# Four-part transformer stack on one core: the products of constants in TensorE's stream are taken out ahead of the last unit

## The chip, the cores and the metric

The kernel runs on one core of one Trainium2 chip. The core has a matrix engine (TensorE, PE in the rows, its weight loads PEld), VectorE (DVE), ScalarE (ACT), GpSimd (POOL) and SyncE (SP), which issues most transfers. Each engine works through its own list of instructions in order and waits on semaphores for the others. The metric is the device time of one execution in microseconds (us), lower is better; the median of several executions is what is compared.

## The reference

Four blocks follow each other on x of shape (4, 1024, 256), all in float32, each as x = x + layernorm(block(layernorm(x))):

```python
def _encoder_layer(x, Wq, ..., ln2_b):                 # block 1: four of these, linear attention, 16 heads
    h = _layernorm(x, ln1_s, ln1_b)
    q, k, v = [(h @ W + b).reshape(b, t, H, DK) ...]
    qp, kp = jax.nn.elu(q) + 1.0, jax.nn.elu(k) + 1.0
    kv = jnp.einsum('bshd,bshm->bhmd', kp, v); ksum = jnp.sum(kp, axis=1)
    z = 1.0 / (jnp.einsum('blhd,bhd->blh', qp, ksum) + EPS_ATTN)
    attn = jnp.einsum('blhd,bhmd,blh->blhm', qp, kv, z).reshape(b, t, d)
    x = x + (attn @ Wo + bo)
    h = _layernorm(x, ln2_s, ln2_b)
    return x + jax.nn.relu(h @ W1 + b1) @ W2 + b2
# block 2: gate = softmax(x @ gate_w.T); out = x @ weight.T + (1/16) * sum over 8 adapters of gate * (x U^T) V^T
# block 3: Mamba: x @ W_in, causal conv of 4, silu, a recurrence over time with 16 states for each of 512 channels
def step(h, inp):
    u, d, b, c = inp
    h = h * jnp.exp(d[..., None] * A) + (d * u)[..., None] * b[:, None, :]
    return (h, jnp.einsum('bds,bs->bd', h, c))
# block 4: top-1 mixture of 8 experts (256 -> 1024 -> 256), up to 320 tokens in each, weighted by the gate
```

## The kernel before

**Tiling.** The 4096 tokens are four batches `b` of 1024, each in four groups `g` of 256 rows. Batch by batch the four encoder layers `l` run on the groups (64 groups of work in all), then block 2 (`mix`), and the result goes to DRAM. Block 3 works in eight units `u` of 512 tokens, two for each batch: its input products (`unit_input`), 64 steps (16 states times 4 channel tiles: ACT makes the decay at L1736, DVE scans at L1233 and multiplies at L1245, POOL makes products at L1991 and adds at L2004), then its output, its gate and the sorting of tokens to experts (`unit_output`). The units of batch b run beside the encoder of batch b+1. Units 6 and 7 have no encoder beside them; there TensorE adds the step's products itself (L825). When the last unit is done, the eight experts run (`expert_up`, `expert_down`).

**Order.** Each engine's list is fixed when the program is built. The work is written as generators that yield due times out of tables of numbers (`ENC`, `BASE_A`, `UNIT`, `OUT_PE` and so on), and `weave` always lets the generator with the earliest due time write its next piece. Nothing is decided on the chip: an engine that meets an unmet semaphore stands, and all behind it stands too.

**The products of constants.** Some pieces of TensorE's stream start with `n` products of the identity with itself, written into the PSUM bank that the piece has just been given and overwritten by it. Nothing reads them. They come after the wait for the bank and ahead of the wait for the data:

```python
def transposes(bank, src, order, freed, ready, spare=0):
    if freed:
        pe.wait_ge(*freed)
    idle(spare, bank)
    for semaphore, value in ready:
        pe.wait_ge(S(semaphore), value)
    for m, (t, k) in enumerate(order):
        ins = pe.transpose(bank[:, m * 128:(m + 1) * 128], src[:, t, k * 128:(k + 1) * 128], C["ident"][:])

def idle(n, bank):
    for _ in range(n):
        pe.matmul(bank[:, 0:128], C["ident"][:], C["ident"][:], start=True, stop=True, skip_group_check=True)
```

The identity is a slice of `pack0`, so the rows call them L461, `ps<-sb_pack`, and each float32 product is two records there (a transpose, L455, is one). Their numbers stand in tables, one entry for a batch and group or for a unit. `WARM_AT` stands ahead of the first product of queries with `kvm` (L602) of a group, in each of the four layers; `WARM_TR2` ahead of the transposes of the attention's result (`attended`, L455); `WARM_TR3` ahead of the transposes for the feed-forward part; `WARM_MIX` and `WARM_MIX3` (group 3) in `mix`, at its first transposes, ahead of L706 and ahead of the transposes at L718; `WARM_IN` ahead of the transposes of a unit's input (L455 on `sb_px`); `WARM_OUT` and `WARM_TR1` are all zero; `WARM_END` stands behind the last unit.

What the neighbours in the rows are: L583 sums keys times values into the bank from which DVE masks `kvm` (L1090, L1094); L1112 on DVE is the attention's result `sb_xh`, normed; L1488 on ACT is the last step of a layernorm, on which the transposes wait; L1867 on POOL is the same for a unit's input `sb_px`; L680 is the feed-forward's second product; L468 is the three-part product of split float32 operands (`mm3`).

Of the kernel before, what the change touches and what calls it, by code (L numbers as in the profile page):

```python
# [125 lines left out]
LATE = NU - 2  # L126

WARM_TR1 = ((0, 0, 0, 0), (0, 0, 0, 0), (0, 0, 0, 0), (0, 0, 0, 0))
WARM_AT = ((4, 3, 0, 0), (8, 1, 0, 0), (4, 0, 0, 0), (4, 0, 0, 0))
WARM_TR2 = ((0, 0, 1, 0), (0, 0, 1, 2), (0, 0, 1, 0), (8, 0, 1, 0))  # L130
WARM_TR3 = ((0, 0, 0, 0), (0, 0, 0, 0), (0, 0, 0, 0), (2, 0, 0, 0))
WARM_MIX = ((6, 0, 2, 0), (7, 0, 2, 0), (7, 0, 2, 0), (11, 0, 2, 0))
WARM_MIX3 = ((6, 4, 0, 0), (6, 0, 0, 0), (6, 0, 0, 0), (8, 0, 0, 0))
WARM_IN = ((6, 0, 0), (6, 0, 0), (6, 0, 0), (4, 0, 0), (6, 0, 0), (6, 0, 0), (6, 0, 0), (7, 0, 0))
WARM_OUT = ((0, 0, 0, 0), (0, 0, 0, 0), (0, 0, 0, 0), (0, 0, 0, 0), (0, 0, 0, 0), (0, 0, 0, 0), (0, 0, 0, 0), (0, 0, 0, 0))
WARM_END = (18, 22, 20, 6, 20, 22)

# [37 lines left out]
def build(nc, a, out):  # L175
    outer = ExitStack()
    with outer:
        sems = {}

        def S(name):  # L180
            if name not in sems:
                sems[name] = outer.enter_context(nc.semaphore("s_" + name))
            return sems[name]
# [182 lines left out]
        def tail(b, g, off):  # L366
            return ENC[b] + (L * LAYER + TAIL[b][g] + TAILS * off) * SLOW[b]
# [28 lines left out]
        def loads(b, n):  # L396
            return 48 * b + 16 * n - (16 if b or n > 1 else 0)
# [48 lines left out]
        def pe_program(pe):  # L446
# [9 lines that stand above are left out]
                return ins  # L456
# [5 lines that stand above are left out]
# [56 lines left out]
            def features(which, pos, when):  # L518
                for b, l, g in groups:
# [6 lines left out]
                                     ((f"d_x{g}", loads(b, 2)) if loaded else (f"lna_g{g}", j + 1),),  # L526
                                     spare=(WARM_TR1 if which == "tr1" else WARM_TR3)[b][g])
                    ins.then_inc(S(which), 1)
# [59 lines left out]
            def attend():  # L588
                for b, l, g in groups:
                    k = place(b, l, g)  # L590
                    for t in range(2):
# [5 lines left out]
                        if t == 0:  # L597
                            idle(WARM_AT[b][g], bank)
                        pe.wait_ge(S("qe"), k + 1)
# [7 lines left out]
            def attended():  # L607
                for b, l, g in groups:
# [3 lines left out]
                    where["tr2", k] = bank  # L612
                    ins = transposes(bank, xh[at(b, g)], by_t, freed, (("an", 2 * k + 2),), spare=WARM_TR2[b][g])
                    ins.then_inc(S("tr2"), 1)
# [70 lines left out]
            def mix(g):  # L685
                for b in range(NB):
                    r, j = 4 * b + g, norm(b, MIX)
                    spare = (WARM_MIX3 if g == 3 else WARM_MIX)[b]
                    yield tail(b, g, 0.0) + MIXED[b][0]
# [47 lines left out]
            def unit_input():  # L737
                for u in range(NU):
                    for k in range(2):
# [3 lines left out]
                        ins = transposes(bank, pxs[u], [(t, k) for t in range(4)], freed,  # L743
                                         (("lnp_p", 3 * u + 3), ("lna_p", 2 * u + 2)), spare=WARM_IN[u][0] if k == 0 else 0)
                        ins.then_inc(S("win"), 1)
                        ring.give(bank, S("pt"), 2 * u + k + 1)
                    for c in range(4):
# [5 lines left out]
                        if c == 0:  # L753
                            idle(WARM_IN[u][1], bank)
                        pe.wait_ge(S("pt"), 2 * u + 2)
# [21 lines left out]
                    if freed:  # L777
                        pe.wait_ge(*freed)
                    idle(WARM_IN[u][2], bank)
                    pe.wait_ge(S("xi"), 8 * u + 8)  # L780
# [1679 lines left out]
```

## Time and profile before

| | |
|---|---|
| median of 3 runs | 2798.64 us |
| lowest, highest | 2791.62, 2802.93 us |
| profiled execution, first to last instruction (span) | 2801.1 us |
| TensorE / weight loads busy | 85% / 70% of the span |
| DVE / POOL / ACT busy | 65% / 62% / 58% |
| granted TensorE clock, mean | 0.921 |
| products of constants, all | 924 records, 462 instructions |
| of these behind 2616 us | 216 records, 108 instructions |

The profiled execution is one execution, and its span lies 2.5 us above the median of the runs. Busy shares are of the whole span; TensorE's count a product from its start to its modelled end, so neighbouring products overlap in them, and the distance from one start to the next is what a product takes from the engine's time. PEclk is the clock that TensorE was granted, 1.00 being 2.4 GHz and 0.50 being 1.2 GHz.

### The profile page before, as it was taken

The numbers are of one execution on the slowest core, as the hardware profiler recorded it, in microseconds if no ns is written. First come the engines' busy times: TensorE is split into PE (matmuls) and PEld (weight loads), VectorE is DVE, ScalarE is ACT, GpSimd is POOL, SyncE is SP. The second block draws the span as 40 slices with busy tenths as digits, with TensorE's granted clock in tenths as the row PEclk, the third lists the DMA queues.
The fourth block names the chain that finished last, engine by engine and source line by source line (L and its number), as shares of the span: only waits on it lengthen the run. The fifth ranks groups of instructions, "written<-read, shape, count | busy, mean of one in ns | idle before, by whom it ended". The sixth has DMA issues, their size and how long they took to land. (4 is left out here: it accounts for less than half of the span.)

```text
span 2801.1 us, 40293 instructions
## 1 busy us (share of the span) xinstructions
PE 2391.1 (85%) x13172; PEld 1965.7 (70%) x13172; DVE 1810.1 (65%) x3883; ACT 1618.4 (58%) x3649; POOL 1723.6 (62%) x1988
## 2 busy tenths in 40 slices
PE   6999998899989858798989887989898766666898
PEld 5889987687869755686878756877788532122698
DVE  4232334678677774887378667784777766879566
ACT  4555666677656654666476655766666556523153
POOL 1111214298659873898369847985598755778356
PEclk8999999999979988899999998999999878778899
DMA  4435233223413232232223133232221232323142
GB/s 159 170 139 192 95 116 135 92 63 104 120 63 95 69 120 88 72 112 66 100 65 113 50 132 100 77 114 74 78 91 46 72 119 73 81 81 88 47 146 93
DMA packets 123899, 273.85 MB, mean 98 GB/s; under 512 B 9213, under 2 KB 64125, under 8 KB 114092
## 3 DMA queue, kind: packets, MB, share of 16 engines
q1 hardware_dynamic: 120108, 263.37, 29.4%
q0 software_dynamic: 3584, 7.92, 0.8%
q8 instruction: 107, 1.75, 0.3%
q14 instruction: 100, 0.82, 0.1%
HBM read 215.93 MB, written 58.48 MB: 98 GB/s over the span
## 5 line engine op out<-in xcount | busy, mean ns | idle before, releaser
L1991 POOL TENSOR_TENSOR sb_sc<-sb_bc,sb_du 128x512 f32<-128x512 f32 x512 | 660.8, 1296 | 107.6 <-issue 38.3
L2004 POOL TENSOR_TENSOR sb_ya<-sb_ya,sb_sc 128x512 f32<-128x512 f32 x384 | 494.8, 1289 | 27.3 <-DVE sb_sc L1245 27.1
L680 PE MATMUL ps<-sb_w,sb_fa 128*128 128x256 f32 x2048 | 494.2, 385 | 5.2 <-ACT sb_fa L1601 5.2
L468 PE MATMUL ps<-sb_hT,sb_w 128*128 128x256 f32 x2048 | 405.2, 297 | 15.7 <-issue 5.9
L680 PEld LDWEIGHTS ps<-sb_w,sb_fa 128*128 128x128 f32 x2048 | 376.6, 193 | 49.8 <-ACT sb_fa L1601 3.9
L1736 ACT ACTIVATE ps<-sb_dl,sb_aneg 128x512 f32<-128x512 f32 x512 | 349.9, 687 | 99.3 <-DVE sb_sc L1245 91.0
L1233 DVE TENSOR_TENSOR_SCAN ps<-ps,sb_sc 128x512 f32<-128x512 f32 x240 | 292.9, 1224 | 101.5 <-ACT ps L1736 94.1
L468 PEld LDWEIGHTS ps<-sb_hT,sb_w 128*128 128x128 f32 x2048 | 329.2, 193 | 34.5 <-issue 23.2
L1233 DVE TENSOR_TENSOR_SCAN ps<-ps,sb_hl,sb_sc 128x512 f32<-128x512 f32 x240 | 306.8, 1283 | 67.2 <-ACT ps L1736 63.2
L1245 DVE TENSOR_TENSOR sb_sc<-ps,sb_bc 128x512 f32<-128x512 f32 x480 | 321.8, 671 | 0.0
L1601 ACT ACTIVATE sb_fa<-ps,sb_b1n 128x256 f32<-128x256 f32 x512 | 209.8, 464 | 147.3 <-PE ps L468 146.9
L468 PE MATMUL ps<-sb_hL,sb_w 128*128 128x256 f32 x1024 | 292.4, 286 | 0.0
L1876 POOL TENSOR_SCALAR sb_g_rs<-sb_g_ss 128x2 f32<-128x2 f32 x148 | 30.1, 204 | 323.0 <-ACT sb_xh L1480 316.8
L825 PE MATMUL ps<-sb_sc,sb_pack 128*128 128x512 f32 x256 | 160.8, 745 | 76.5 <-DVE sb_sc L1245 61.6
L455 PE MATMUL ps<-sb_pack,sb_xh 128*128 128x128 f32 x832 | 134.9, 289 | 101.6 <-ACT sb_xh L1488 86.5
L468 PE MATMUL ps<-sb_wq,sb_hT 128*128 128x512 f32 x512 | 198.9, 430 | 19.7 <-DVE sb_b1n L1026 7.6
L1488 ACT ACTIVATE sb_xh<-sb_xb,sb_g_nm,sb_g_rs 128x256 f32<-128x256 f32 x304 | 164.9, 591 | 75.4 <-POOL sb_g_nm L1883 74.7
L468 PEld LDWEIGHTS ps<-sb_hL,sb_w 128*128 128x128 f32 x1024 | 196.3, 192 | 0.0
L455 PEld LDWEIGHTS ps<-sb_pack,sb_xh 128*128 128x128 f32 x832 | 105.0, 149 | 125.8 <-ACT sb_xh L1488 64.9
L1060 DVE TENSOR_TENSOR sb_hL<-ps,sb_hT 128x512 fp32r<-128x512 f32 x128 | 87.9, 687 | 141.5 <-ACT sb_hT L1436 140.7
L825 PEld LDWEIGHTS ps<-sb_sc,sb_pack 128*128 128x128 f32 x256 | 49.6, 224 | 182.9 <-DVE sb_sc L1245 131.0
L1878 POOL TENSOR_TENSOR sb_g_rs<-sb_g_rs,sb_mhalf 128x2 f32<-128x2 f32 x184 | 130.7, 710 | 57.1 <-DVE sb_g_nm L981 44.7
(262 smaller groups left out, 5055.1 us busy)
## 6 DMA issues: line engine op xcount, KB each, us to landing
sb_bc<-b_and_c SPq DMA_DIRECT2D x128, 512.0 KB, 5.0
sb_w<-w_parts SPq DMA_DIRECT2D x15, 2048.0 KB, 7.7
sb_wq<-w_qkv_parts SPq DMA_DIRECT2D x15, 1536.0 KB
sb_w<-in_w SPq DMA_DIRECT2D x16, 1024.0 KB
sb_raw<-in_mw SPq DMA_DIRECT2D x16, 1024.0 KB, 9.7
gate_z<-sb_xin SPq DMA_DIRECT2D x30, 256.0 KB, 2.2
sb_zt<-gate_z SPq DMA_DIRECT2D x30, 256.0 KB, 3.8
expert_in<-sb_bb SPq DMA_DIRECT2D x5, 1032.0 KB, 12.9
```

What stands on the lines that cost most here:

```text
L455: ins = pe.transpose(bank[:, m * 128:(m + 1) * 128], src[:, t, k * 128:(k + 1) * 128], C["ident"][:])
L468: ins = pe.matmul(bank, lhs[x], rhs[y], start=(first and m == 0), stop=(last and m == 2), skip_group_check=True)
L680: ins = pe.matmul(acc[:, v * D:(v + 1) * D], fa[i % 3][:, h * 256 + v * 128:h * 256 + (v + 1) * 128], w2[:, 2 * f + h, :], start=(f == 0 a ...
L825: pe.matmul(held[c][:], C["ident"], db[m % RING], start=False, stop=(s == NS - 1), skip_group_check=True).then_inc(S("adp"), 1)
L1233: v.tensor_tensor_scan(db[m % RING] if on_pool(m) else da[m % 3][:], da[m % 3][:], db[m % RING], start, ALU.mult, ALU.add).then_inc(S("sc" ...
L1245: v.tensor_tensor(db[m % RING], da[m % 3][:], bc[:, i % 3, 1, :], ALU.mult).then_inc(S("cm"), 1)
L1488: ins = e.activation(xh[at(b, g)][:, t, :], x[:, t, :], ACT.Identity, bias=nm[:, t:t + 1], scale=rs[:, t:t + 1])
L1601: ins = e.activation(fa[i % 3][:, cols], where["w1", i][:, cols], ACT.Relu, bias=b1n[:, l, 2 * f + h2:2 * f + h2 + 1])
L1736: e.activation(da[m % 3][:], dls[u][:, c, :], ACT.Exp, scale=aneg[:, c, s:s + 1]).then_inc(S("ex"), 1)
L1878: i = own.tick(p.tensor_tensor(rs[:, 0:2], rs[:, 0:2], mhalf[:, 0:2], ALU.pow))
L1991: p.tensor_tensor(db[m % RING], bc[:, i % 3, 0, :], dus[u][:, c, :], ALU.mult).then_inc(S("bm"), 1)
L2004: p.tensor_tensor(yas[u][:, c, :], yas[u][:, c, :], db[m % RING], ALU.add).then_inc(S("ad"), 1)
```

## The change

Six of the nine tables are set to zero: `WARM_AT`, `WARM_TR2`, `WARM_TR3`, `WARM_MIX`, `WARM_MIX3` and `WARM_IN`. `WARM_END` is kept. No due time and no other instruction is touched; where a block of L461 carried the wait for its bank, the first instruction behind it now carries that wait.

```diff
-WARM_AT = ((4, 3, 0, 0), (8, 1, 0, 0), (4, 0, 0, 0), (4, 0, 0, 0))
-WARM_TR2 = ((0, 0, 1, 0), (0, 0, 1, 2), (0, 0, 1, 0), (8, 0, 1, 0))
-WARM_TR3 = ((0, 0, 0, 0), (0, 0, 0, 0), (0, 0, 0, 0), (2, 0, 0, 0))
-WARM_MIX = ((6, 0, 2, 0), (7, 0, 2, 0), (7, 0, 2, 0), (11, 0, 2, 0))
-WARM_MIX3 = ((6, 4, 0, 0), (6, 0, 0, 0), (6, 0, 0, 0), (8, 0, 0, 0))
-WARM_IN = ((6, 0, 0), (6, 0, 0), (6, 0, 0), (4, 0, 0), (6, 0, 0), (6, 0, 0), (6, 0, 0), (7, 0, 0))
+WARM_AT = ((0, 0, 0, 0), (0, 0, 0, 0), (0, 0, 0, 0), (0, 0, 0, 0))
+WARM_TR2 = ((0, 0, 0, 0), (0, 0, 0, 0), (0, 0, 0, 0), (0, 0, 0, 0))
+WARM_TR3 = ((0, 0, 0, 0), (0, 0, 0, 0), (0, 0, 0, 0), (0, 0, 0, 0))
+WARM_MIX = ((0, 0, 0, 0), (0, 0, 0, 0), (0, 0, 0, 0), (0, 0, 0, 0))
+WARM_MIX3 = ((0, 0, 0, 0), (0, 0, 0, 0), (0, 0, 0, 0), (0, 0, 0, 0))
+WARM_IN = ((0, 0, 0), (0, 0, 0), (0, 0, 0), (0, 0, 0), (0, 0, 0), (0, 0, 0), (0, 0, 0), (0, 0, 0))
 WARM_END = (18, 22, 20, 6, 20, 22)
```

TensorE's stream in the first layer of batch 0, where the queries of groups 0 and 1 meet `kvm` (`s_qe` and `s_ke` are the waits for a bank, `s_kvm` the one for the masked sums):

```order
-L461 MATMUL ps<-sb_pack 128x128 [waits s_qe]
-L461 MATMUL ps<-sb_pack 128x128 x3
 L602 MATMUL ps<-sb_kvm,sb_xh 128x136 [waits s_kvm,s_qe]
 L602 MATMUL ps<-sb_kvm,sb_xh 128x136
 L602 MATMUL ps<-sb_kvm,sb_xh 128x136 [waits s_kvm,s_qe,s_ke]
 L602 MATMUL ps<-sb_kvm,sb_xh 128x136
-L461 MATMUL ps<-sb_pack 128x128 [waits s_ke]
-L461 MATMUL ps<-sb_pack 128x128 x2
-L602 MATMUL ps<-sb_kvm,sb_xh 128x136 [waits s_kvm,s_qe]
+L602 MATMUL ps<-sb_kvm,sb_xh 128x136 [waits s_kvm,s_qe,s_ke]
```

The seven products are gone, and the wait for the bank `s_ke` moved onto the L602 behind them; the L602 products follow each other in the same order.

TensorE's stream in a layer of batch 3, where the attention's result of group 0 is transposed (`s_an` counts DVE's L1112):

```order
 L602 MATMUL ps<-sb_kvm,sb_xh 128x136 [waits s_kvm,s_qe,s_an]
 L602 MATMUL ps<-sb_kvm,sb_xh 128x136
-L461 MATMUL ps<-sb_pack 128x128 [waits s_an]
-L461 MATMUL ps<-sb_pack 128x128 x7
 L455 MATMUL ps<-sb_pack,sb_xh 128x128 [waits s_an]
 L455 MATMUL ps<-sb_pack,sb_xh 128x128 x3
```

Eight products are gone between the last L602 and the transposes, and the wait stays the same one.

## Rows read from the trace of the kernel before

**Rows 1.** The cores' clock; the page's busy time and clock in 40 slices
```profile
core 0: 2801.1 us, clock 0.921
...
PE 2391.1 (85%) x13172; PEld 1965.7 (70%) x13172; DVE 1810.1 (65%) x3883; ACT 1618.4 (58%) x3649; POOL 1723.6 (62%) x1988
...
PEclk8999999999979988899999998999999878778899
```

**Rows 2.** Busy time by stretch, all engines; the column after POOL is PEclk
```profile
0.00:434.00 434.00, 403.62 (x2488) 358.92 (x2489) 145.43 (x496) 240.02 (x613) 77.00 (x201) 0.96 0.40 144
550.00:960.00 410.00, 376.18 (x2229) 330.15 (x2229) 307.07 (x603) 267.68 (x641) 323.29 (x339) 0.95 0.28 86
2330.00:2616.00 286.00, 197.61 (x380) 71.27 (x379) 235.08 (x300) 130.34 (x218) 213.26 (x196) 0.84 0.29 80
```

**Rows 3.** Line L461 alone: the whole line, and the last stretch (PE, PEld, PEclk)
```profile
L461 PE MATMUL ps<-sb_pack x924: 270/275/584, 60.7 to 2657.8; 128*128 128x128 f32 x185
...
2616.00:2801.00 185.00, 29.02 (x216) 28.21 (x216) 0.95 0.30 106
```

**Rows 4.** Order of time, layer 0 of batch 0: start, us, what, [idle before]
```profile
60.75 1.06 PE L461 MATMUL ps<-sb_pack 128*128 128x128 f32 x8
...
61.35 0.17 DVE L1094 TENSOR_TENSOR sb_kvm<-ps,sb_pack 128x16 f32<-128x16 f32 x1
...
61.67 1.17 PE L602 MATMUL ps<-sb_kvm,sb_xh 128*128 128x136 f32 x8
...
62.68 0.83 PE L461 MATMUL ps<-sb_pack 128*128 128x128 f32 x6
...
63.34 0.51 PE L602 MATMUL ps<-sb_kvm,sb_xh 128*128 128x136 f32 x3
```

**Rows 5.** Order of time, end of batch 0's encoder
```profile
433.06 1.08 ACT L1488 ACTIVATE sb_xh<-sb_xb,sb_g_nm,sb_g_rs 128x256 f32<-128x256 f32 x2
...
434.05 1.50 PE L461 MATMUL ps<-sb_pack 128*128 128x128 f32 x12
...
435.38 0.60 PE L455 MATMUL ps<-sb_pack,sb_xh 128*128 128x128 f32 x4
```

**Rows 6.** Order of time, layer of batch 3
```profile
1737.89 0.75 DVE L1112 TENSOR_TENSOR sb_xh<-ps,sb_zz 128x256 f32<-128x256 f32 x2
...
1739.08 2.23 PE L461 MATMUL ps<-sb_pack 128*128 128x128 f32 x16
...
1741.15 0.60 PE L455 MATMUL ps<-sb_pack,sb_xh 128*128 128x128 f32 x4
```

**Rows 7.** Order of time, input of unit 2
```profile
1053.13 1.09 POOL L1867 TENSOR_SCALAR sb_px<-sb_px,sb_p_rs,sb_p_nm 128x256 f32<-128x256 f32 x2
...
1054.35 2.77 PE L461 MATMUL ps<-sb_pack 128*128 128x128 f32 x12
...
1056.90 1.09 PE L455 MATMUL ps<-sb_pack,sb_px 128*128 128x128 f32 x8
```

**Rows 8.** Order of time on PE: waits behind blocks of L461
```profile
651.21 1.95 PE L461 MATMUL ps<-sb_pack 128*128 128x128 f32 x16
654.73 1.16 PE L602 MATMUL ps<-sb_kvm,sb_xh 128*128 128x136 f32 x8 [1.57 <-DVE sb_kvm L1094]
...
1260.14 2.09 PE L602 MATMUL ps<-sb_kvm,sb_xh 128*128 128x136 f32 x16 [2.91 <-DVE sb_kvm L1094]
...
1298.96 1.61 PE L455 MATMUL ps<-sb_pack,sb_px 128*128 128x128 f32 x8 [2.96 <-POOL sb_px L1867]
...
1733.51 5.78 PE L602 MATMUL ps<-sb_kvm,sb_xh 128*128 128x136 f32 x24 [2.77 <-DVE sb_kvm L1094]
```

**Rows 9.** Busy time by stretch, PE alone, right behind waits (PE busy, PEclk)
```profile
654.70:658.10 3.40, 3.24 (x26) 1.00 0.87 332
...
1260.10:1263.50 3.40, 3.01 (x24) 1.00 0.65 239
...
1733.50:1739.10 5.60, 5.59 (x25) 0.50 0.91 283
...
1299.00:1302.40 3.40, 3.40 (x14) 0.55 0.72 204
```

## The prediction

> **What bounds the kernel now.** I read the page first, then the stretches, then the order of time around each block of L461. On the page TensorE is busy 85% of the span and nobody else over 65% [rows 1], but shares over the whole span do not say who is late where. By stretch there are three regimes [rows 2]. Up to 434 us TensorE is busy 404 of 434 us and VectorE a third of it: TensorE's stream alone sets the time. From 550 to 2330, where the encoder of the next batch runs beside two units, TensorE is busy about 90% (376 of 410 in its first part) and POOL and VectorE about 75% to 80%: the end runs back and forth between TensorE, the layernorms on ACT, POOL and VectorE and the scans, and each is late in turn. From 2330 to 2616 VectorE (235 of 286) leads, and there is no L461. The page's chain of waits reaches back only to the last 200 us, so ahead of that I judge each block by its neighbours: had the data behind it come before it ended, or did TensorE stand after it as well?
>
> The second thing to read is the clock. The mean granted clock of the span is 0.921 [rows 1]. With two levels, 1.00 and 0.50, that is (1 - 0.921) / 0.5 = 0.158 of the span, some 440 us, at 1.2 GHz. The slices at 0.7 and 0.8 are those where TensorE has gaps, the slices at 0.9 the dense ones [rows 1].
>
> **What is removed.** 462 products stand in 924 records; 216 records lie behind 2616 us and stay [rows 3]. 708 records, 354 products, go. At full clock a record takes 0.11 us of the engine's time: six records from 62.68 to 63.34 [rows 4]. So 708 x 0.11 = 78 us of TensorE's time go, near 2.8% of the span. That is not the gain, and each block is one of two kinds.
>
> *Blocks that fill a wait.* At 60.75 eight records run until 61.67, and the `kvm` on which the product behind them waits is done at 61.35 + 0.17 = 61.52 [rows 4]. Without them TensorE stands instead, and starts no more than 0.1 us sooner. At 651.21 sixteen records are followed by a further wait of 1.57 us for the same `kvm` [rows 8]. Taking these away frees nothing. By going through all of nearly 90 blocks I count some 45 us of the 78 here: cover is the wait itself.
>
> *Blocks that hold up work that is ready.* I add up min(length of the block, end of the block minus arrival of the data):
> - Layers of batch 0: the second block, 62.68 to 63.34, stands before queries that need only the `kvm` of 61.52 [rows 4]. 0.67 us, in four layers, plus a few tenths: 3 us.
> - The end of batch 0's encoder: the layernorm is done at 434.14, the transposes start at 435.38 [rows 5], and 1.2 us is lost. Seven blocks of 4 to 12 records between 434 and 491 are like this, 0.4 to 1.3 us each: 6.6 us. TensorE feeds unit 0 from here, so it counts in full.
> - The layers of batch 3: group 0's result is done within 1737.89 + 0.75 = 1738.64, sixteen records run from 1739.08 to 1741.15 [rows 6]. 2.07 us here and 1.8 us in each of the other three layers: 7.5 us.
> - Inputs of units and parts of `mix`: 1054.35 to 1056.90 with `sb_px` ready at 1054.22 [rows 7], 2.55 us, and four smaller ones: 5 us.
>
> The sum that lies on a line of work which nothing else overtakes is 22 us. Some 13 us more of the same kind (2 to 4 records each, in batches 1 and 2) lie where another engine is late just after, and I count them as nothing. Between TensorE and the others there is little slack in the shared stretches, and a part of the 22 us is met there by a wait for ACT, POOL or DVE: I take 80%, **18 us less**, with 12 and 22 as ends.
>
> **What it costs.** The rows behind waits show it [rows 8, 9]. Behind the wait of 1.57 us at 654.73 the clock is 1.00. Behind 2.77 us at 1733.51 it is 0.50 for the whole 5.6 us of the query products, and behind 2.96 us at 1298.96 it is 0.55 over the next 3.4 us. Behind 2.91 us at 1260.14 it stayed at 1.00, so near 3 us it can go either way. Twenty-four records of L602 between 1733.51 and 1739.08 take 0.232 us each [rows 6, 8]; eight between 61.67 and 62.68 take 0.126 at full clock [rows 4]. At the lower level the same products take nearly twice the time. So 3.4 us spent at 0.50 is 1.7 us of work lost, and 5.6 us is 2.8.
>
> The change lengthens the wait behind nearly every filling block, by 0.45 to 2.5 us. I count twelve places where the clock now stays at 1.00 and the wait becomes 3 to 4 us, as at 654.73, where 1.57 becomes 1.57 + 16 x 0.11 = 3.3 us, longer than both waits behind which the clock is seen at half [rows 8]. At 1.7 us each that is 20 us. In some five more places the block itself was what TensorE did ahead of the clock's return while it was at the lower level (the sixteen records at 1739 and the twelve at 1054 [rows 6, 7] cost 2.07 and 2.55 us there and are followed by faster work); without them dense work has to do it, at half speed, 1.7 to 2.8 us each: 11 us. Work behind these waits is what the rest was waiting for, so most of it is on the path; again 80% of 31 is **25 us more**. Its ends are wide: 6 us if only a third of the places drop, 45 if the low stretches last as at 1733.51 and the places that drop already stay low for longer too.
>
> The Trainium skill speaks to the same point twice (TensorE: Matmul & The Clock Gate, in "HAM oscillation — how this bites in real kernels"): the lower clock is the default, and idle stretches between bursts give it back. By that rule the waits above should be filled, and the change makes the kernel slower; the trace agrees as far as rows 8 and 9 go. The same page (Part 1) says that for modelling the ramp penalty is under 1% of a typical span, an estimate of under 28 us here; the trace has some 440 us at half clock, far more than that, so I do not use it as a bound.
>
> **The sum.** -18 + 25 = +7 us. The profiled execution's span is 2801.1, 2.5 us over the median; the difference is carried to the median unchanged: 2798.6 + 7 = 2806 us, 0.25% slower.
>
> **The rivals.**
> 1. *The clock wins.* If the low stretches last 5.6 us rather than 3.4 us and the engines beside TensorE, which are at 75%, cannot catch up, the cost is 17 x 2.8 x 0.8 = 38 us and the losses of the other waits, say 5, come to it. Against the gain of 18 that is +25 us: 2824. It decides from the point where more than half of the dropped places stay low for longer than 3.4 us. For it: each wait in the shared stretches is a wait for a result that itself came from TensorE a few us before, so a slow stretch begets a longer wait. Against: dense work follows most of these waits, and over all the slices of the shared stretches the clock is at 0.9 [rows 1], so it comes back soon each time.
> 2. *Only the held-up work counts.* If the lengthened waits mostly do not drop the clock (as behind 1260.14), 22 us less and 6 us more leave -16 us: 2783.
> 3. *Nothing moves.* The blocks are slack on both sides, for the held-up work only arrives at the next wait sooner, and the clock falls where it falls already. 2798. That TensorE meets waits for ACT, POOL and DVE of some us behind many blocks [rows 8] speaks for it; the 404 of 434 us of the first stretch [rows 2] speak against.
>
> That the change does not do what it says is no rival: the stream of TensorE loses the blocks and nothing else.
>
> **How the numbers follow.** The sum, 2806, has 45%; its own range, by the ends of its terms taken half-way, is 2795 to 2817. Rival 1 has 30%, rival 2 has 15%, rival 3 has 10%. A measurement of this kernel can tell about 0.5% from no change, 14 us: 2785 to 2813. Rival 2 lies just under it and gives most of the 0.14 for faster. Of the sum 80% lie within, and rival 3 whole: with bits of rival 1 and 2, 0.49. Slower takes most of rival 1 and a fifth of the sum: 0.37. The range goes from 2784, which leaves out half of rival 2, to 2834, above rival 1 by the end of its price (45 us and a gain of 12 would be 2832).
>
> **What would show it.** In the profile after, L461 should stand at 216 records, all behind 2616. If the sum is right the mean clock falls from 0.921 to 0.91 or 0.90 (17 more places of 3.4 us at half are 58 us, which is 0.01, and up to 0.02 if they last longer); the queries behind the waits for `kvm` at about 654, 918 and 1260 run at half clock; the end of batch 0's encoder (the first transposes of `mix`, now 435.38) comes 3 us sooner, and unit 0's input another 6 us sooner; and the gain is eaten up between 550 and 2330. The first step would be wrong if these come at the same times as before. The second would be wrong if the mean clock stays at 0.92. A gain that lasts to the start of the last two units (2330) would make the whole wrong.

## The result, and the profile after

| | before | after |
|---|---|---|
| median | 2797.12 us (4 runs) | 2809.53 us (4 runs) |
| lowest, highest | 2791.62, 2802.93 | 2806.57, 2811.77 |
| ratio to before, 95% interval | | 1.0045 [1.0029, 1.0062] |
| span of the profiled execution | 2801.1 | 2809.8 |
| mean granted clock | 0.921 | 0.900 |
| at half clock, (1 - mean) / 0.5 x span | 442 us | 562 us |

The changed kernel is 0.45% slower, about 12 us (8 to 17 by the interval). The forecast was 7 us and 2806.

The last row is for one execution each. Every later run measured before again beside its own kernel, 71 times in all. These executions have a mean clock of 0.924 and 422 to 431 us at half clock, by group, so the profiled one, at 0.921 and 442, is at the slow end. The four of after have a mean of 0.9015, 553 us at half clock. The change adds some 120 to 130 us of it.

The page after, as in rows 1, and the line of the products of constants, as in rows 3:

```profile
span 2809.8 us, 38934 instructions
...
PE 2352.7 (84%) x12464; PEld 1911.9 (68%) x12464; DVE 1808.6 (64%) x3883; ACT 1619.1 (58%) x3649; POOL 1724.0 (61%) x1988
...
PEclk8999998999979878899989987999999778878899
...
L461 PE MATMUL ps<-sb_pack x216: 273/275/580, 2624.6 to 2666.4; 128*128 128x128 f32 x108
```

TensorE does 708 records less, and the kernel is slower. VectorE, ScalarE and POOL do what they did.

TensorE's busy time by stretch (start:end, us, busy, PEclk, DMA), after:

```profile
0.00:434.00 434.00, 399.66 (x2458) 0.96 0.40 144
434.00:550.00 116.00, 89.89 (x413) 0.85 0.37 123
550.00:960.00 410.00, 371.12 (x2125) 0.93 0.28 87
...
1530.00:1670.00 140.00, 108.27 (x526) 0.84 0.31 92
...
2150.00:2330.00 180.00, 118.76 (x424) 0.75 0.26 82
2330.00:2600.00 270.00, 182.01 (x335) 0.83 0.30 84
```

The first stretch has the same clock as in rows 2, the second regime less (0.93 for 0.95 from 550 to 960). The largest falls are at the ends of the batches, where the encoder of one batch gives way to the next. Before, these stretches had:

```profile
434.00:550.00 116.00, 96.37 (x509) 0.93 0.37 125
...
1530.00:1670.00 140.00, 113.84 (x612) 0.90 0.30 91
...
2150.00:2330.00 180.00, 127.79 (x549) 0.81 0.27 80
```

The waits of rows 8, in order of time on TensorE, and the clock behind the first of them:

```profile
648.58 4.69 PE L602 MATMUL ps<-sb_kvm,sb_xh 128*128 128x136 f32 x24 [3.35 <-DVE sb_kvm L1094]
...
913.20 5.57 PE L602 MATMUL ps<-sb_kvm,sb_xh 128*128 128x136 f32 x24 [3.73 <-DVE sb_kvm L1094]
...
1260.34 4.40 PE L602 MATMUL ps<-sb_kvm,sb_xh 128*128 128x136 f32 x24 [3.80 <-DVE sb_kvm L1094]
...
648.50:651.90 3.40, 3.32 (x15) 0.54 0.94 342
```

The wait of 1.57 us at 654.73 has become 3.35 us, and behind it the clock is 0.54 instead of 1.00 [rows 8, 9]. The one of 2.91 us at 1260.14 is now 3.80, and its 24 records take 4.40 us, 0.18 us each: between the 0.126 of full clock and the 0.232 of half, since the clock came back during them.

The waits of TensorE between 550 and 2330, after and then before (engine, line, waited for, total, times, longest):

```profile
PE ps L455 <- ACT sb_xh L1488: 100.6, 23, 21.7
PE ps L602 <- DVE sb_kvm L1094: 30.2, 10, 3.8
```
```profile
PE ps L455 <- ACT sb_xh L1488: 75.0, 19, 20.4
PE ps L602 <- DVE sb_kvm L1094: 19.6, 9, 2.9
```

These two waits alone grew by 36 us. In this stretch 561 records had been taken out, 62 us at 0.11 us each, so more than half of that came back as standing in these two waits.

Where the time goes is best seen by marks. The end of the same instruction is read in two profiled executions, and the table has the difference to before in us; the kernels of the experiments are in it already. "Mix 0" is the last result of block 2 for batch 0 (494.8 before), "unit 0", "unit 7" the last of the unit's output (815.5, 2630.4), "enc 1" to "enc 3" the last sum of the feed-forward part of that batch's encoder (1028.1, 1629.5, 2209.7).

| kernel | mix 0 | unit 0 | enc 1 | enc 2 | enc 3 | unit 7 |
|---|---|---|---|---|---|---|
| after | -7.8 | -5.2 | -1.0 | +1.1 | +6.9 | +8.2 |
| fill | -7.0 | -5.9 | -3.9 | -4.6 | -8.1 | -11.6 |
| hold | -2.9 | +0.6 | +4.7 | +8.6 | +8.5 | +7.0 |
| narrow | -7.0 | -4.5 | -0.2 | +1.5 | +2.1 | -1.1 |
| more2 | -7.9 | -6.7 | -4.9 | -9.9 | -12.5 | -15.6 |
| more2n | -8.6 | -3.2 | -0.2 | +4.0 | +10.0 | +10.7 |
| tail0 | -2.1 | -3.5 | -3.3 | -3.6 | -3.5 | -6.7 |

Single executions of one kernel differ by up to 0.3% and more, and the one of before is a slow one (2801.1, where its medians are 2795 to 2797). So the rows read some us too favourable at their end; the table tells where things happen, and the ratios how large they are. After leads by 7.8 us when batch 0 is through and has lost 16 us by the last unit.

### The profile page after: what moved, and what is told of

It is laid out like the page before. It is cut to its first block and busy times, and to the rows that moved or that the text cites. A ratio compares the mean times of both kernels' runs of the same rounds, so it can differ in the third digit from the quotient of the medians.

```text
span 2809.8 us, 38934 instructions
## 1 busy us (share of the span) xinstructions
PE 2352.7 (84%) x12464; PEld 1911.9 (68%) x12464; DVE 1808.6 (64%) x3883; ACT 1619.1 (58%) x3649; POOL 1724.0 (61%) x1988
## 3 DMA queue, kind: packets, MB, share of 16 engines
q8 instruction: 102, 1.67, 0.2%
## 5 line engine op out<-in xcount | busy, mean ns | idle before, releaser
L1488 ACT ACTIVATE sb_xh<-sb_xb,sb_g_nm,sb_g_rs 128x256 f32<-128x256 f32 x304 | 164.9, 591 | 78.6 <-POOL sb_g_nm L1883 78.2
```

Source lines behind the costliest of these rows:

```text
L1488: ins = e.activation(xh[at(b, g)][:, t, :], x[:, t, :], ACT.Identity, bias=nm[:, t:t + 1], scale=rs[:, t:t + 1])
```

## The experiments

The working theory was the one of the prediction: blocks in front of ready work cost, blocks in front of a wait pay, and pay by the clock. Its rivals: what is freed is lost at the next wait and the clock has little part in it; or the time moves with the timetable and has no pattern.

**The two kinds apart.** *fill* keeps the 196 products in front of waits and takes out the 158 in front of ready work; *hold* does the opposite.

```diff
 # fill
+WARM_AT = ((4, 0, 0, 0), (8, 0, 0, 0), (4, 0, 0, 0), (4, 0, 0, 0))
+WARM_TR2 = ((0, 0, 0, 0), (0, 0, 0, 0), (0, 0, 0, 0), (0, 0, 0, 0))
+WARM_MIX = ((0, 0, 0, 0), (7, 0, 0, 0), (7, 0, 0, 0), (6, 0, 0, 0))
+WARM_MIX3 = ((6, 0, 0, 0), (6, 0, 0, 0), (6, 0, 0, 0), (8, 0, 0, 0))
+WARM_IN = ((0, 0, 0), (6, 0, 0), (0, 0, 0), (4, 0, 0), (0, 0, 0), (6, 0, 0), (6, 0, 0), (0, 0, 0))
 # hold
+WARM_AT = ((0, 3, 0, 0), (0, 1, 0, 0), (0, 0, 0, 0), (0, 0, 0, 0))
+WARM_TR3 = ((0, 0, 0, 0), (0, 0, 0, 0), (0, 0, 0, 0), (0, 0, 0, 0))
+WARM_MIX = ((6, 0, 2, 0), (0, 0, 2, 0), (0, 0, 2, 0), (5, 0, 2, 0))
+WARM_MIX3 = ((0, 4, 0, 0), (0, 0, 0, 0), (0, 0, 0, 0), (0, 0, 0, 0))
+WARM_IN = ((6, 0, 0), (0, 0, 0), (6, 0, 0), (0, 0, 0), (6, 0, 0), (0, 0, 0), (0, 0, 0), (7, 0, 0))
```

> The kernel before less only those products of constants that hold up work whose data is there (158 of the 354 instructions; 196 stay, all in front of a wait that outlasts them). Theory 1 (the change gains by freeing TensorE and loses by the clock): the gain without the loss, 8 to 18 us faster than before, 2780 to 2789, mean clock 0.91 to 0.92. Theory 2 (what is freed is lost again at the next wait, the clock has little part): within 4 us of before. Theory 3 (a shifted timetable, no pattern): anywhere within 8 us of before, either side.

> The complement: only the 196 products that fill a wait are taken out, the 158 in front of ready work stay. Theory 1: the loss without the gain, slower than the changed kernel: 17 to 28 us over before, 2814 to 2825, mean clock near 0.90. Theory 2: like the changed kernel, 2806 to 2812. Theory 3: within 8 us of before.

Measured: fill 0.9984 [0.9971, 0.9997], 4.5 us faster; hold 1.0043 [1.0031, 1.0055], 12 us slower. The signs are those of theory 1, and the intervals exclude a common value. Both sizes are short of it: 4.5 us where 8 to 18 was expected, 12 where 17 to 28 was. Theory 2 fits these two sizes better: it had fill within 4 us of before and hold at 2806 to 2812, where 2808 was measured. So the clock needed a test of its own. One thing speaks for it already: the ten executions of fill have a mean clock of 0.918, 456 us at half clock, 34 more than before beside it. The products in front of ready work had held the clock up too.

**Width against place.** *narrow* is fill with each filler 4 columns wide instead of 128 (the ones behind the last unit stay wide).

```diff
-pe.matmul(bank[:, 0:128], C["ident"][:], C["ident"][:], ...)
+pe.matmul(bank[:, 0:cols], C["ident"][:], C["ident"][:, 0:cols], ...)   # cols = 4, or 128 for WARM_END
```

> The kernel that keeps the 196 filling products, with each of them 4 columns wide instead of 128; same instructions, same places, same weight loads (the single-column products of L513 show 0.13 us a record at full clock in the trace of before, so they hold TensorE as long). Theory 1 (the fillers work through the clock): the load of weights alone does not keep the clock, so the loss of the changed kernel comes back: 2803 to 2812, mean clock near 0.90, the waits for kvm followed by half clock. Theory 2 (they work by where they put TensorE's stream in time, not by the clock): as the kernel with the wide ones, 2788 to 2796, with the same clock.

Measured: 1.0030 [1.0016, 1.0043], against 0.9984 for the wide ones: 13 us for the width alone. The order of time on TensorE and the clock behind the wait, fill and then narrow:

```profile
644.26 1.95 PE L461 MATMUL ps<-sb_pack 128*128 128x128 f32 x16
647.78 2.09 PE L602 MATMUL ps<-sb_kvm,sb_xh 128*128 128x136 f32 x16 [1.56 <-DVE sb_kvm L1094]
...
647.70:651.10 3.40, 2.97 (x23) 1.00 0.91 340
```
```profile
645.89 1.85 PE L461 MATMUL ps<-sb_pack 128*128 128x4 f32 x16
649.40 4.69 PE L602 MATMUL ps<-sb_kvm,sb_xh 128*128 128x136 f32 x24 [1.67 <-DVE sb_kvm L1094]
...
649.40:652.80 3.40, 3.40 (x15) 0.51 0.89 335
```

The block holds the engine nearly as long (1.95 and 1.85 us), the wait left behind it is nearly as long (1.56 and 1.67), and the queries come out at full clock in the one and at half in the other. This is the case against theory 2, and against theory 3 as well, for the stream and its places are the same. Narrow fillers leave nearly the time of the changed kernel, which has none (1.0030 and 1.0045, and their intervals overlap): of the 17 us between fill and after, 13 are the width, and the other 4 are within the noise.

The same was done for the longest fillers (*more2*, below, and *more2n*).

> The kernel with the longest fillers so far, each of them 4 columns wide. Theory 1 (the fillers work by the clock): the gain of that kernel goes and the loss of the changed one comes, 2800 to 2812, clock near 0.905, though TensorE's stream and its durations at full clock are the same. Theory 2: 2780 to 2790, like the wide ones.

Measured: 1.0062 [1.0046, 1.0077], where the wide ones have 0.9959 [0.9942, 0.9976]. The factor between them is 1.0103, 29 us. At the same place, more2 and then more2n:

```profile
644.25 3.29 PE L461 MATMUL ps<-sb_pack 128*128 128x128 f32 x28
647.77 2.09 PE L602 MATMUL ps<-sb_kvm,sb_xh 128*128 128x136 f32 x16 [0.23 <-DVE sb_kvm L1094]
...
647.70:651.10 3.40, 2.98 (x23) 1.00 0.89 339
```
```profile
647.06 3.19 PE L461 MATMUL ps<-sb_pack 128*128 128x4 f32 x28
650.58 4.69 PE L602 MATMUL ps<-sb_kvm,sb_xh 128*128 128x136 f32 x24 [0.33 <-DVE sb_kvm L1094]
...
650.50:653.90 3.40, 3.32 (x17) 0.61 0.92 334
```

Here TensorE stands for a third of a microsecond only in both, and behind the narrow fillers the clock is at half for most of the 3.4 us all the same.

**Longer fillers.** *more* and *more2* start from fill and lengthen the blocks that leave a wait behind them (330 and 366 products in all).

```diff
 # more
+WARM_AT = ((4, 0, 0, 0), (11, 0, 0, 0), (10, 0, 0, 0), (10, 0, 0, 0))
+WARM_TR3 = (..., (8, 0, 0, 0));  WARM_MIX = ((0, 0, 0, 0), (12, 0, 0, 0), (10, 0, 0, 0), (8, 0, 0, 0))
+WARM_IN = ((0, 0, 0), (8, 0, 0), (0, 0, 0), (12, 0, 0), (0, 0, 0), (10, 0, 0), (12, 0, 0), (0, 0, 0))
 # more2
+WARM_AT = ((4, 0, 0, 0), (14, 0, 0, 0), (8, 0, 0, 0), (12, 0, 0, 0))
+WARM_TR3 = (..., (10, 0, 0, 0));  WARM_MIX as in more
+WARM_IN = ((0, 0, 0), (8, 0, 0), (0, 0, 0), (16, 0, 0), (0, 0, 0), (14, 0, 0), (20, 0, 0), (0, 0, 0))
```

> As the first, with the blocks in front of waits made longer where a wait of 1.5 us or more is left behind them (330 products in all, none in front of ready work as the trace of before has it). Theory 1: the mean clock rises over 0.92 and the time falls under that of the first kernel by 3 to 8 us, unless the longer blocks now overrun the wait in some layer. Theory 2 and 3: as the first kernel or slower, by up to 5 us, since TensorE has more to do.

> Still longer fillers (14, 8 and 12 at kvm in batches 1, 2 and 3, where the kernel with longer fillers had 11, 10 and 10; 16 to 20 instead of 12 at the inputs of units 3 and 6). Theory 1: 2778 to 2788, as the one before or some us less, until blocks overrun the wait of the layer in which it is shortest. Theory 2: slower than the one before by 2 to 6 us, since TensorE has more to do.

Measured: more 0.9957 [0.9941, 0.9974], 2783.25 us; more2 0.9959 [0.9942, 0.9976], 2784.61 us. Both beat the kernel before by 0.4% and the changed one by 0.9%. The step from 330 to 366 products brings nothing more. The expectation had more 3 to 8 us under fill; it is 7.5 by the ratios. The profiled execution of more had 2792.8 us and a clock of 0.921, but it is the odd one of four: the others took 2781.7 to 2783.6 us at 0.927 to 0.929, where before had 0.924. The six of more2 have 0.925 to 0.929.

**Which places.** *at_only* keeps of fill's blocks only those in front of `kvm`, *rest_only* only the others.

```diff
 # at_only: fill, and
+WARM_TR3, WARM_MIX, WARM_MIX3, WARM_IN: all zero
 # rest_only: fill, and
+WARM_AT: all zero
```

> Of the 196 fillers only the 80 in front of the queries' wait for kvm stay. Theory 1: the loss is spread over the places, 2797 to 2803. If the loss is made at the ends of the batches alone, where waits of 2 to 20 us stand: as the changed kernel, 2806 to 2812. If it is made in the layers: as the kernel with all 196, 2788 to 2795.

> The other 116 fillers stay (at the ends of the batches, at the inputs of units and two in each layer of batch 3), those at kvm go. Theory 1, spread: 2797 to 2803. Loss at the batches' ends: 2788 to 2795. Loss in the layers: 2806 to 2812.

Measured: 1.0018 [1.0008, 1.0028] and 1.0008 [0.9991, 1.0025]. Over fill they lose 0.34% and 0.24%; over fill, after loses 0.61%. Both medians (2802 and 2800) lie in the 2797 to 2803 expected for a loss that is spread over both kinds of place, roughly by halves.

**A new place.** *tr3_b12* is before with fillers ahead of the layernorm for the feed-forward part of group 0 in batches 1 and 2, where TensorE stands 3 to 5.6 us. *most* is more2 with these and with fillers at the transposes of three units' outputs.

```diff
 # tr3_b12
+WARM_TR3 = ((0, 0, 0, 0), (6, 0, 0, 0), (12, 0, 0, 0), (2, 0, 0, 0))
 # most: more2, and
+WARM_TR3 = ((0, 0, 0, 0), (6, 0, 0, 0), (12, 0, 0, 0), (10, 0, 0, 0))
+WARM_OUT[u][1] = 6, 6, 20 for u = 0, 2, 5
```

> Before with fillers at a new place, in front of the wait for the first layernorm ahead of the feed-forward part, 6 in the layers of batch 1 and 12 in those of batch 2, where TensorE stands 3 to 5.6 us and the clock falls behind it. Theory 1: 3 to 8 us faster than before, and fewer stretches at half clock between 550 and 1530. Theory 2: same or slower by up to 3 us.

> The longest fillers with this new place and three more in front of the transposes of units' outputs (6, 6 and 20 at units 0, 2 and 5). Theory 1: 2774 to 2784, mean clock 0.93 or more. Theory 2: 2784 to 2792.

Measured: 0.9997 [0.9985, 1.0008] and 0.9963 [0.9950, 0.9977]. The spans and mean clocks of tr3_b12 and then of most:

```profile
core 0: 2786.5 us, clock 0.931
```
```profile
core 0: 2785.2 us, clock 0.932
```

The clock rose to the highest of all, and the time did not move for it. Over all their executions, tr3_b12 has 28 us less at half clock than before beside it (398 for 425), and most has 38 us less than more2 (372 for 410). The first was to gain 3 to 8 us, and its interval is 4 us faster to 2 us slower; most, at 2784.6, is just outside its 2774 to 2784. Theory 1 in the form "more at full clock is faster" fails here: the fillers at this place work on the clock, and the time hardly answers. Whether what runs behind them is not what the others wait for, or the 72 added products cost what the clock gives, was not tested.

**The gain, term by term.** *tail0* is before without the 34 products at the end of batch 0's encoder; *tr2b3* is before without the eight ahead of the transposes in batch 3.

```diff
 # tail0
+WARM_MIX[0] = (0, 0, 0, 0);  WARM_MIX3[0] = (6, 0, 0, 0);  WARM_IN[0] = (0, 0, 0)
 # tr2b3
+WARM_TR2 = ((0, 0, 1, 0), (0, 0, 1, 2), (0, 0, 1, 0), (0, 0, 1, 0))
```

> Before with only the products that hold up ready work at the end of batch 0's encoder taken out (34 instructions; mix of batch 0 and the input of unit 0), the term that stood for 6.6 us of the predicted gain. If the term was right: 5 to 7 us faster than before, and the whole of it still there at the end. If what is gained there is met by the next wait: 2 to 4 us at the start of unit 0, and that or less at the end. If it is lost by the clock: under 1 us, with a longer stretch at half clock between 434 and 550.

> Before with one entry at zero: the eight products in front of the transposes of group 0 in the four layers of batch 3, which stood for 7.5 us of the predicted gain. Theory 1 as predicted: 5 to 7.5 us faster, unless the clock falls at that place. Theory 2: within 2 us of before. If the products there pay for themselves by the clock: slower by 1 to 5 us, and the clock between 1740 and 2110 lower than before.

Measured: tail0 0.9989 [0.9979, 1.0000], 3 us faster where its term was 6.6; tr2b3 0.9989 [0.9978, 1.0001], 3 us where its term was 7.5. The intervals reach to 6 us for both, and to nothing. The size of tail0 is that of the middle expectation, a gain met by the next wait, but its trace shows the third at work as well, the clock. The transposes of `mix` of group 0 and of group 3 in it, and behind them group 3 before:

```profile
434.19 0.63 PE L455 MATMUL ps<-sb_pack,sb_xh 128*128 128x128 f32 x4
...
480.21 1.11 PE L455 MATMUL ps<-sb_pack,sb_xh 128*128 128x128 f32 x4 [7.69 <-ACT sb_xh L1488]
```
```profile
482.27 1.12 PE L455 MATMUL ps<-sb_pack,sb_xh 128*128 128x128 f32 x4 [8.29 <-ACT sb_xh L1488]
```

The first transposes come 1.19 us sooner than at 435.38 [rows 5], as the term said, those of group 2 3.1 us, and those of group 3 only 2.1 us: they wait for a layernorm (L1488) whose chain through POOL, VectorE and ACT came 2.05 us sooner and no more. The clock took its part on the way. The products behind the removed blocks in tail0, and the same ones before:

```profile
467.14 3.18 PE L728 MATMUL ps<-sb_pack,sb_xh 128*128 128x256 f32 x8
...
486.68 1.91 PE L455 MATMUL ps<-sb_pack,sb_px 128*128 128x128 f32 x8
488.38 2.81 PE L728 MATMUL ps<-sb_pack,sb_xh 128*128 128x256 f32 x8
```
```profile
468.92 1.89 PE L728 MATMUL ps<-sb_pack,sb_xh 128*128 128x256 f32 x8
...
490.51 1.04 PE L455 MATMUL ps<-sb_pack,sb_px 128*128 128x128 f32 x8
491.38 1.89 PE L728 MATMUL ps<-sb_pack,sb_xh 128*128 128x256 f32 x8
```

The lead is 2.1 us at group 3's transposes, 3.8 us at those of unit 0's input (486.68 for 490.51), where two more blocks are gone, and 2.1 us again behind L728: here the removed blocks gained 1.8 us, and the lower clock took the same back at once. In tr2b3 the four transposes of the place in rows 6, and the next wait; then the same wait before:

```profile
1738.12 0.89 PE L455 MATMUL ps<-sb_pack,sb_xh 128*128 128x128 f32 x4
...
1751.35 0.66 PE L455 MATMUL ps<-sb_pack,sb_xh 128*128 128x128 f32 x4 [3.54 <-ACT sb_xh L1488]
```
```profile
1752.77 0.66 PE L455 MATMUL ps<-sb_pack,sb_xh 128*128 128x128 f32 x4 [2.21 <-ACT sb_xh L1488]
```

At 1741.15 before and 1738.12 here the lead is 3.03 us, of which 1.0 had been there before the place (the wait for `kvm` ends at 1732.55 instead of 1733.51). Eleven us later it is 1.42: of the 2.07 us of the block 0.5 are left, and the wait is 1.33 us longer. Over the whole of batch 3 the lead of tr2b3 grows by 4.0 us, from 0.9 at enc 2 to 4.9 at enc 3, of the 7.5.

## Why the prediction was right, and where it was not

**What bounds the kernel.** As said: until 434 us TensorE, then all engines in turn. The marks show the gain of the first stretch and its loss in the shared ones.

**The blocks that hold up ready work.** The term that was too large is the -18, the 80% of 22 us. The rows of the sum each hold, but all 158 such products together bring 4.5 us (fill, 1 to 8 by its interval), two terms of 6.6 and 7.5 us bring 3 us each. What comes out is a fifth to a half. Two things are missing from the 80%, and the runs do not divide the shortfall exactly. One is the next wait: I had seen that the data behind each block was there, and had not followed the work one wait further, to a layernorm whose own chain does not come sooner by the same amount (tr2b3: 2.07 us of the block, 0.5 left). The other is the clock: these blocks too were what TensorE did ahead of dense work, and without them that runs slower (tail0: 1.8 us gained and lost within one group). Fill's 34 us more at half clock are, at the price found below, an estimate of 6 to 7 us, so without this loss fill would have gained some 11.

**The blocks that fill a wait.** The mechanism was right, shown by width alone (13 and 29 us), the size was not: 25 us were forecast, hold shows 12. The 17 places were not counted again one by one. Between the profiles of before and after the time at half clock rose by 120 us, where the prediction had 58 for its 17 places, and up to twice that, so its time was at the upper end. What was too high is the price of each us at half clock. Over the means of all executions, 97 us more at half clock from fill to after cost 17 us, 78 from fill to narrow 13, 72 from before to hold 12, and 129 from more2 to more2n 29: 0.17 to 0.22 us for each. I had taken 0.5 x 80% = 0.4. The spread within one kernel is of the same order: over the 71 later executions of before, 0.25 us for each us at half clock, though that alone does not say which causes which.

The five places at which the block itself ran at the lower level were put at 1.7 to 2.8 us each, and at both that it names the clock costs less. At 1739 the clock was back after 0.7 us of the block's 2.07 (1.00 from 1739.8 on), and in tr2b3 the transposes there take 0.89 us for 0.60, 0.3 us lost. At 1054 the block is at 0.50 throughout, and in after the transposes in its place take 1.77 us for 1.09, 0.7 us lost:

```profile
1053.46 1.77 PE L455 MATMUL ps<-sb_pack,sb_px 128*128 128x128 f32 x8
```

**The sum.** +7 came from two terms, both too large by a factor of two to four, and their errors cancelled; +12 was measured. That the number came so near was luck. (The sum's own range, by ends taken half-way, comes to 2794 to 2819 rather than 2795 to 2817.) Fill and hold add up to +7.5 us, 5 us short of +12, which the intervals of the three ratios allow to be nothing. The marks put the rest into batch 3: hold, which still has the eight products at the transposes, stays at +8.5 from enc 2 to enc 3, and after goes from +1.1 to +6.9. There the blocks in front of ready work seem to do the fillers' part when these are gone. This was not tested by itself, and single executions differ by as much.

**The rivals.** Rival 1 (2824, +25) is too dear, though the time at half clock rose by more than its 17 x 5.6 = 95 us. Rival 2 (2783) and rival 3 (2798) are excluded by the interval of 8 to 17 us slower.

**The signs.** All of those named came: 216 records, all behind 2616; a mean clock of 0.900 for 0.91 or 0.90; the queries behind 654, 918 and 1260 at the lower level for most of their time (0.63, 0.53 and 0.67 over each run of 24 records); the gain eaten between 550 and 2330. The first transposes of `mix` came 7.3 us sooner instead of 3:

```profile
428.12 0.63 PE L455 MATMUL ps<-sb_pack,sb_xh 128*128 128x128 f32 x4
```

Of this, 2.9 us have another cause, in the last section. Unit 0's input was to be another 6 us ahead of that and was not: the lead at mix 0 is 7.8.

The Trainium skill (TensorE: Matmul & The Clock Gate, "HAM oscillation — how this bites in real kernels") had the sign right: idle stretches between bursts lose the full clock and should be avoided. (That the lower clock is the default stands in its Part 1.) Its estimate of under 1% is for the ramp up to full clock. No run here shows what all the time at half clock (16% to 20% of the span) costs; what changes in it cost is 0.45% for the change and 1.03% for the width of the longest fillers.

## What to carry to other kernels

Products of constants in front of a wait can pay, and the same products in front of ready work cost: sort the places by whether the engine still stands behind them, take those out behind which it does not, and lengthen the others (0.4% faster here than before). Do not price half clock at half of its time: of each us at half clock 0.17 to 0.22 us came out at the end here, and at the new place of tr3_b12 nothing clear of noise. Even the products in front of ready work had held the clock up, so look for that before counting all of their time as gain. And a freed microsecond is a gain only once it is followed beyond the next wait.

## What the runs showed of the hardware

The clock also fell where TensorE had no gap at all. In batch 0 before, 32 records of one column (the bias products, L513) stand between dense products, with nothing idle; order of time on TensorE, and the clock from 132.00 on:

```profile
127.80 1.89 PE L680 MATMUL ps<-sb_w,sb_fa 128*128 128x256 f32 x8
129.53 4.57 PE L513 MATMUL ps<-sb_pack,sb_ya 128*128 128x1 f32 x32
...
134.53 3.62 PE L680 MATMUL ps<-sb_w,sb_fa 128*128 128x256 f32 x8
...
132.00:138.80 6.80, 6.80 (x24) 0.50 0.97 349
```

And after, where the same instructions stand 1.2 us sooner:

```profile
126.59 1.89 PE L680 MATMUL ps<-sb_w,sb_fa 128*128 128x256 f32 x8
128.32 3.63 PE L513 MATMUL ps<-sb_pack,sb_ya 128*128 128x1 f32 x32
...
132.13 1.89 PE L680 MATMUL ps<-sb_w,sb_fa 128*128 128x256 f32 x8
...
131.00:137.80 6.80, 6.80 (x40) 1.00 1.00 364
```

The same eight products take 3.62 us in one and 1.89 in the other, and behind them the kernel is 2.9 us further than the 1.2 us that it led by. Whether the clock falls there is chance as far as these traces tell: it fell in six of the 14 profiled executions (before, more, tr2b3, tail0, rest_only, and for a shorter time at_only). The stream of tr3_b12 is that of before up to batch 1, and there it did not fall. A part of the spread among executions of one kernel may come from such places.
